# Twelve embedding tables looked up by matmul instead of ten, a 2 KB gather-descriptor ring, 25 chunks of marks, and whole layer parts between the gram pieces

## What is computed

```python
e = jnp.stack([tbl_0[ids[:, 0]], ..., tbl_25[ids[:, 25]]], axis=1)      # (2048, 26, 128)
combined = jnp.concatenate([dense[:, None, :], e], axis=1)              # (2048, 27, 128)
interactions = jnp.einsum('bfd,bgd->bfg', combined, combined)[:, TRIU_I, TRIU_J]   # 351
h = jnp.concatenate([dense, interactions, dense], axis=1)               # (2048, 607)
h = jnp.maximum(h @ W_top1 + b_top1, 0.0)
h = jnp.maximum(h @ W_top2 + b_top2, 0.0)
y = h @ W_top3                                                          # (2048, 1)
```

## Time and profile before

| | before |
|---|---|
| median of 3 runs | 398.69 us (398.37 to 398.92) |
| the profiled execution | 400.2 us, of which 398.3 us is the span of its instructions |
| PE busy / PE weight loads | 364.5 us (92%) / 309.7 us (78%) |
| DVE busy | 261.1 us (66%) |
| POOL busy | 247.2 us (62%), 256 gathers |
| ACT busy | 137.0 us (34%) |
| granted TensorE clock, mean | 0.983 of full speed |
| DMA | 31.72 MB, 80 GB/s on average |

### The profile page before, as it was taken

One profiled execution on the slowest core, in us unless ns is written; L12 is line 12 of the kernel. 1 busy time (PEld: TensorE's weight loads), 2 busy tenths in 40 slices (PEclk: granted clock), 3 DMA queues, 4 the chain that ended last, 5 costly groups with the idle time before them and its releaser, 6 DMA issues.

```text
span 398.3 us, 13947 instructions
## 1 busy us (share of the span) xinstructions
PE 364.5 (92%) x6192; PEld 309.7 (78%) x6192; DVE 261.1 (66%) x748; ACT 137.0 (34%) x195; POOL 247.2 (62%) x260
## 2 busy tenths in 40 slices
PE   0857758999999999999999999999999999999798
PEld 0757747987689977997789876997789877997575
DVE  2999864990699409990599519990699419980310
ACT  3545130343325234323433334323433334324222
POOL 6777777777677665776677666775677666720000
PEclk9998996999999999999999999999999999999989
DMA  7953442223112311323122311313121312200000
GB/s 242 411 195 110 149 144 57 54 55 120 49 42 55 113 43 44 82 53 115 43 55 55 114 49 44 81 54 109 48 51 53 116 47 51 54 22 2 5 2 0
DMA packets 13677, 31.72 MB, mean 80 GB/s; under 512 B 5301, under 2 KB 6205, under 8 KB 13618
## 3 DMA queue, kind: packets, MB, share of 16 engines
q0 software_dynamic: 8192, 16.79, 15.9%
q1 hardware_dynamic: 5426, 14.04, 9.7%
HBM read 30.81 MB, written 0.01 MB: 77 GB/s over the span
## 4 chain that ended last, share of the span: by engine, by line
PE 48%; DVE 44%; issue 4%; DMA 3%; ACT 1%; SPq 0%
DVE marks L580 37%; PE flip_ps L364 12%; PE mlp_ps L412 11%; PE gram_ps L386 9%; PE flip_ps L346 6%; PE mlp_ps L421 5%; PE mlp_ps L415 3%; DVE dots L558 3%; DVE lo L588 3%; DMA feats<-small_rows 1%; DMA id_cols<-ids_in_pairs 1%; DVE pair_dots L566 1%; PE mlp_ps L430 1%; PE pairs_ps L397 1%; ACT feats L622 0%
## 5 line engine op out<-in xcount | busy, mean ns | idle before, releaser
L328 POOL DMA_INDIRECT emb<-tbl,idx x256 | 247.0, 965 | 103.8 <-issue 55.8
L580 DVE TENSOR_SCALAR marks<-id_cols,row_no 125x256 fp32r<-125x256 int16 x688 | 211.5, 384 | 4.9 <-DMA id_cols<-ids_in_pairs 4.9
L364 PE MATMUL flip_ps<-marks,hi 125*128 125x256 f32 x688 | 172.2, 291 | 18.4 <-DVE marks L580 18.0
L364 PE MATMUL flip_ps<-marks,lo 125*128 125x256 f32 x688 | 167.9, 284 | 0.0
L364 PEld LDWEIGHTS flip_ps<-marks,hi 125*128 125x128 f32 x688 | 132.6, 193 | 26.0 <-issue 21.3
L364 PEld LDWEIGHTS flip_ps<-marks,lo 125*128 125x128 f32 x688 | 132.7, 193 | 0.0
L558 DVE STREAM_TRANSPOSE dots<-gram_ps 128x864 f32<-128x864 f32 (+1 forms) x32 | 25.2, 824 | 105.8 <-PE gram_ps L386 105.8
L622 ACT COPY feats<-flip_ps 128x512 f32<-128x512 f32 x40 | 46.7, 1167 | 124.4 <-PE flip_ps L364 119.4
L386 PEld LDWEIGHTS gram_ps<-feats 128*27 128x27 f32 x4096 | 43.0, 106 | 44.4 <-issue 43.3
L544 ACT COPY feats<-flip_ps 128x512 f32<-128x512 f32 x64 | 45.0, 725 | 64.9 <-PE flip_ps L346 62.8
L386 PE MATMUL gram_ps<-feats 128*27 128x27 f32 x4096 | 54.9, 192 | 10.2 <-issue 6.8
(11 more groups left out here) (23 smaller groups left out, 63.6 us busy)
## 6 DMA issues: line engine op xcount, KB each, us to landing
id_cols<-ids_in_pairs SPq DMA_DIRECT2D x7, 640.0 KB
emb<-tbl,idx POOLq DMA_INDIRECT x256, 2.5
feats<-small_rows SPq DMA_DIRECT2D x5, 512.0 KB, 7.5
dense_sb<-dense_columns SPq DMA_DIRECT2D x4, 256.0 KB, 9.2
w1p_sb<-w_pairs SPq DMA_DIRECT2D x1, 702.0 KB
hT<-small_rows SPq DMA_DIRECT2D x1, 640.0 KB, 12.6
w1p_sb<-small_rows SPq DMA_DIRECT2D x1, 640.0 KB, 14.5
dots<-small_rows SPq DMA_DIRECT2D x1, 640.0 KB, 4.0
```

The lines of the kernel that those rows point to most:

```text
L328: nc.gpsimd.indirect_dma_start(emb[:, v, (f - 1) * P:f * P], None, tables[order[f - 1]][:, :], bass.IndirectOffsetOnAxis(ap=idx[:, t, orde ...
L364: last = nc.tensor.matmul(flip_ps[:, m % FLIP_BANKS, 2 * (s % 2):2 * (s % 2) + 2, :], part[s][0:R[s], half * x + c, :], marks[0:R[s], MARK ...
L580: last = nc.vector.tensor_scalar(marks[0:R[s], MARKS_AT[h] + c, :], id_cols[0:R[s], s, :], row_no[0:R[s], s, half * x + c:half * x + c + 1 ...
```

## The change

- LOOKED_UP goes from 10 to 12: two tables with 1250 rows are no longer gathered but looked up. The look-ups of a pair have 106 chunks instead of 86, 14 tables are gathered (groups of 4, 4, 4 and 2), and there are six look-up groups instead of five.
- The SBUF kept for the descriptors of POOL's gathers goes from its default of 16 KB a partition to 2 KB (dynamic_dma_scratch_size).
- The ring of marks goes from 28 to 25 chunks; AHEAD, which follows from it, becomes 6 half-tables (24 chunks), and the half-tables fall to other places of the ring.
- The layers between the gram pieces are no longer cut: the gram pieces stand as piece, flip, piece, and then a whole layer. layer 4 of the last pair but one moves ahead of the last pair's odd gram pieces, and the third layer ahead of the last piece. ACT's order and the list of weighted places follow.

Two tables more than before have to wait for a place at the start: tables 10 and 11 go to the places of tables 7 and 8.

```diff
--- before.py
+++ after.py
...
 GROUP = 4
-LOOKED_UP = 10
+LOOKED_UP = 12
...
-MARK_CHUNKS = 28
+MARK_CHUNKS = 25
...
             places = [looks(h) for h in range(HALVES)] + part_of_layers(0)
-            places += [piece(even, 0)] + flips(odd, 0) + [piece(even, 1), piece(even, 2)] + flips(odd, 1)
-            places += part_of_layers(1) + [piece(even, 3), piece(even, 4)] + flips(odd, 2) + [piece(even, 5)]
-            places += part_of_layers(2) + [piece(even, 6)] + flips(odd, 3) + [piece(even, 7)] + part_of_layers(3)
-            places += [piece(odd, 0)] + flips(following, 0) + [piece(odd, 1)] + part_of_layers(4)
-            places += [piece(odd, 2)] + flips(following, 1) + [piece(odd, 3), piece(odd, 4)] + flips(following, 2)
-            places += part_of_layers(5) + [piece(odd, 5), piece(odd, 6)] + flips(following, 3)
-            return places + [piece(odd, 7)] + part_of_layers(6)
+            for k in range(GROUPS):
+                places += [piece(even, 2 * k)] + flips(odd, k) + [piece(even, 2 * k + 1)] + part_of_layers(k + 1)
+            places += [piece(odd, 0)] + flips(following, 0) + [piece(odd, 1)] + flips(following, 1)
+            places += [piece(odd, 2), piece(odd, 3)] + part_of_layers(H1C + 1) + [piece(odd, 4)]
+            places += flips(following, 2) + [piece(odd, 5)] + flips(following, 3) + [piece(odd, 6)]
+            return places + part_of_layers(H1C + H2C) + [piece(odd, 7)]
...
-            def layer(i, q, parts=range(4)):
+            def layer(i, q):
...
-                for c in parts:
-                    if q < H1C and c < CHUNKS:
-                        last = nc.tensor.matmul(bank, w1p_sb[0:CHUNK, c, q * P:(q + 1) * P],
-                                                xT[0:CHUNK, c, :, :], start=(c == 0), stop=False)
-                    elif q < H1C:
-                        last = nc.tensor.matmul(bank, w1d_sb[:, q * P:(q + 1) * P],
-                                                dense_sb[:, i % DENSE_PAIRS, :], start=False, stop=True)
-                    else:
+                if q < H1C:
+                    for c in range(CHUNKS):
+                        nc.tensor.matmul(bank, w1p_sb[0:CHUNK, c, q * P:(q + 1) * P],
+                                         xT[0:CHUNK, c, :, :], start=(c == 0), stop=False)
+                    last = nc.tensor.matmul(bank, w1d_sb[:, q * P:(q + 1) * P],
+                                            dense_sb[:, i % DENSE_PAIRS, :], start=False, stop=True)
+                else:
+                    for c in range(H1C):
                         if q == H1C:
 
                             pe.wait_ge(s_act, STEPS * i + c + 1)
                         last = nc.tensor.matmul(bank, w2_sb[:, c, (q - H1C) * P:(q - H1C + 1) * P],
                                                 h1T[:, c, :], start=(c == 0), stop=(c == H1C - 1))
-                if 3 in parts:
-                    last.then_inc(s_mm, 1)
-
-            def third_layer(i, parts=range(H2C)):
-                for c in parts:
+                last.then_inc(s_mm, 1)
+
+            def third_layer(i):
+                for c in range(H2C):
 
                     pe.wait_ge(s_act, STEPS * i + H1C + c + 1)
                     last = nc.tensor.matmul(mlp_ps[0:1, 0, 0:2 * P], w3_sb[:, c:c + 1], h2T[:, c, :],
                                             start=(c == 0), stop=(c == H2C - 1))
-                if H2C - 1 in parts:
...
                 layer(i - 1, 0)
-                gram(2 * i, 0)
-                flip(2 * i + 1, 0)
-                layer(i - 1, 1, range(0, 1))
-                gram(2 * i, 1)
-                layer(i - 1, 1, range(1, 3))
-                gram(2 * i, 2)
-                flip(2 * i + 1, 1)
-                layer(i - 1, 1, range(3, 4))
-                gram(2 * i, 3)
-                layer(i - 1, 2, range(0, 2))
-                gram(2 * i, 4)
-                flip(2 * i + 1, 2)
-                layer(i - 1, 2, range(2, 3))
-                gram(2 * i, 5)
-                layer(i - 1, 2, range(3, 4))
-                layer(i - 1, 3, range(0, 1))
-                gram(2 * i, 6)
-                flip(2 * i + 1, 3)
-                layer(i - 1, 3, range(1, 2))
-                gram(2 * i, 7)
-                layer(i - 1, 3, range(2, 4))
+                for k in range(GROUPS):
+                    gram(2 * i, 2 * k)
+                    flip(2 * i + 1, k)
+                    gram(2 * i, 2 * k + 1)
+                    if k + 1 < H1C:
+                        layer(i - 1, k + 1)
 
             def odd_gram(i):
 
@@ -478,27 +460,22 @@
                     if i + 1 >= EARLY:
                         flip(2 * i + 2, k)
 
-                layer(i - 1, 4, range(0, 2))
+                layer(i - 1, H1C)
                 gram(2 * i + 1, 0)
                 next_flip(0)
-                layer(i - 1, 4, range(2, 3))
                 gram(2 * i + 1, 1)
+                next_flip(1)
+                gram(2 * i + 1, 2)
                 pair_rows(2 * i)
-                layer(i - 1, 4, range(3, 4))
-                gram(2 * i + 1, 2)
-                next_flip(1)
-                layer(i - 1, 5, range(0, 1))
                 gram(2 * i + 1, 3)
-                layer(i - 1, 5, range(1, 3))
+                layer(i - 1, H1C + 1)
                 gram(2 * i + 1, 4)
                 next_flip(2)
-                layer(i - 1, 5, range(3, 4))
                 gram(2 * i + 1, 5)
-                third_layer(i - 1, range(0, 1))
+                next_flip(3)
                 gram(2 * i + 1, 6)
-                next_flip(3)
+                third_layer(i - 1)
                 gram(2 * i + 1, 7)
-                third_layer(i - 1, range(1, 2))
 
...
 
+            layer(last - 1, H1C)
             for part in range(PIECES):
                 gram(tiles - 1, part)
                 if part == 3:
                     pair_rows(tiles - 2)
-            layer(last - 1, 4)
-            layer(last - 1, 5)
+            layer(last - 1, H1C + 1)
             pair_rows(tiles - 1)
...
-                activate(i - 1, range(0, 1))
-                keep_all(2 * i + 1, range(0, 2))
-                activate(i - 1, range(1, 2))
-                keep_all(2 * i + 1, range(2, 3))
-                activate(i - 1, range(2, 3))
-                keep_all(2 * i + 1, range(3, GROUPS))
-                activate(i - 1, range(3, H1C))
+                for k in range(GROUPS):
+                    activate(i - 1, range(k, k + 1))
+                    keep_all(2 * i + 1, range(k, k + 1))
+                activate(i - 1, range(H1C, H1C + 1))
                 if i + 1 < pairs:
                     if i + 1 >= EARLY:
-                        keep_all(2 * i + 2, range(0, 1))
+                        keep_all(2 * i + 2, range(0, 2))
                     keep_pairs(2 * i)
-                    activate(i - 1, range(H1C, H1C + 1))
-                    if i + 1 >= EARLY:
-                        keep_all(2 * i + 2, range(1, 3))
                     activate(i - 1, range(H1C + 1, H1C + H2C))
                     if i + 1 >= EARLY:
-                        keep_all(2 * i + 2, range(3, GROUPS))
+                        keep_all(2 * i + 2, range(2, GROUPS))
                     keep_y(i - 1)
             keep_pairs(tiles - 2)
-            activate(pairs - 2, range(H1C, H1C + H2C))
+            activate(pairs - 2, range(H1C + 1, H1C + H2C))
...
-    nc = bacc.Bacc("TRN2", target_bir_lowering=False, num_devices=1)
+    nc = bacc.Bacc("TRN2", target_bir_lowering=False, num_devices=1, dynamic_dma_scratch_size=2048)
```

More of the change, by code:

```diff
@@ L82, in tower @@
     AHEAD = max(h for h in range(1, HALVES + 1) if sum(SIZES[:h]) <= MARK_CHUNKS)
-    assert CHUNKS == 3 and H1C == 4 and H2C == 2 and GROUPS == 4
+    assert H1C == GROUPS == 4 and H2C == 2 and PIECES == 2 * GROUPS
     ctx = ExitStack()
```

4 lines of the change are left out of this document (2 added, 2 removed).

## The result

The changed kernel takes 457.98 us (median of 4 runs, 456.77 to 458.80) against 398.81 us before (398.37 to 399.10): a ratio of 1.148, 95% interval 1.145 to 1.151. The prediction was 454.5 us with a range of 440 to 467. The profiled execution took 458.29 us, its span is 456.4 us, 58.1 us more than before.

The account below looks back on a forecast made before the run. PE and DVE were taken as balanced in the look-ups, PE alone as the bound elsewhere. Start +18.5, pairs 3 to 6 look-ups 4 x 5.9 and smaller terms sum to +55.8 us: 454.5 us, range 440 to 467.

Parts of the forecast that it names:

- The price of a mark: DVE's marks: 0.261 us for a mark by itself, plus 0.19 us for each gather beside the marks.
- Rival 2: DVE's marks: 0.31 us each however few gathers there are, some +10 us, 464 us; chance 0.18.
- the look-up parts of pairs 3 to 6: Steady pairs: look-up part 27.55 us against 21.64, +5.9 us a pair, bounded by DVE.
- about 13 beside the marks: Look-up part of pairs 3 to 6: 14.6 gathers fall into it, about 13 beside DVE's marks, adding 2.5 us.
- The stop: Start: DVE stands from 41.75 to 51.75 us, until PE has looked up table 6; 10 of the start's +18.5 us.
- Pair 1: Pair 1: 90 marks instead of 70 remain, 25.8 us, look-up part +4.0 us; its gram part +0.15.
- The even tile: Gram part, even tile: from 11.9 to 12.55 us on PE with half a layer more in it, +0.65.
- The tail: After the last odd tile: half of layers 4 and 5's 5.3 us lies in the wait for DVE's transposes, -2.6 us.
- Rival 1: Start: no stop of DVE or a short one, -10 us, 444 us; chance 0.14.
- rival 3: POOL's descriptor ring holds one gather: 96 us a pair for POOL, over 700 us; chance 0.03.
- rival 4: POOL's gathers set the pair, so fewer gathers gain up to 5.0 us a pair, 364 us; chance 0.02.
- rival 5: Two tables looked up but nothing else moved, DVE hidden everywhere: +35 us, 434 us; chance 0.03.

Follow-up runs that it names:

- a lead of 1.0: The changed kernel with PACE_LEAD = 1.0 instead of 0.7 of a pair for the gathers; 457.53 us, ratio 1.149 to the kernel before.
- the exchange of loads: The changed kernel with pair 1's row numbers asked for ahead of the weights of layers 1 and 2 in SP's queue; 458.58 us, ratio 1.153.

## Why the prediction was right, and where it was off

**The mechanism.** DVE's marks end the look-up parts: in pairs 3 to 7 they are done 1.34 us before the look-ups, the 1.35 of the prediction. But they do so by little. With ten tables and a ring of 42 chunks, where PE waits for no mark, the part takes 21.0 us. With twelve tables one part is PE's alone too: in pair 7 of the kernel with a lead of 1.0 the 82 marks take 21.6 us, PE waits for none, and the part takes 25.34 us. So PE's own work accounts for 4.3 us of the 4.6 to 5.4 by which the part grew, and against the 26.2 to 27.1 us of pairs 3 to 6 DVE costs 0.9 to 1.7 us a pair, the most that marks made earlier could give back. No run with twelve tables does that.

**The price of a mark** held: 22.58 us for 82 marks is 82 x 0.261 and 6 gathers of 0.2, and with no gather beside them (pair 7 with the lead of 1.0) 82 marks take 21.63 us, 0.264 each. In the records of the changed kernel 5 or 10 marks of such a run are longer than the others, by 0.14 to 0.21 us (a record of 342 ns becomes one of up to 544), where a gather falls on them. Rival 2, a mark of 0.31 us however few gathers there are, would have needed 25.4 us for 82 marks; 22.6 and 23.4 were measured, with 6 and 11 gathers beside them. The kernel with one late gather shows the same price: 8 gathers fewer beside 58 marks made them 1.8 us faster (16.25 us for 18.04). So against the Trainium skill (SBUF — State Buffer, SBUF: two separate sides), by which a VectorE instruction with one SBUF input, outside the two-port modes, and GpSimd don't block each other, both directions are seen here: 0.2 us of a mark for each gather, and gathers of 8 to 14 us.

**The term that was too big: the look-up parts of pairs 3 to 6.** Predicted 4 x 5.9 = 23.6 us, measured 4.6, 5.4, 4.6 and 5.4. The wrong step is "about 13 beside the marks": only 6 or 11 gathers met them, as one gather was shut out for the rest of the run. 7 gathers are 1.4 us, 2 are 0.4. What looks like harm (POOL busy 35 us longer) is what spares DVE 3.6 us, since PE did not yet wait for the gathers; in the kernel with the late gather it did, and lost 2.8 to 3.0 us in two pairs.

**The start.** The stop: 9.73 us for 10, its two ends within 0.3 us (42.03 and 51.76 for 41.75 and 51.75). Marks done at 66.35, predicted 65.75. The load behind it was 1.1 us longer than the 5.5 + 0.4 of the working, as much as the exchange of loads took away.

**The term that was left out: the gram after the start.** I had put it at nothing. It is 2.1 us, one more hole of 2 us among its matmuls. The clock of 0.50 isn't the reason, since the kernel before has it there too. I had allowed for such holes in the steady odd tiles and not in the first one.

**Pair 1.** +5.3 us for +4.0. Its 90 marks cost what they should (25.3 us for 25.8). The failed step is that the ring of 25 doesn't stop DVE, which the working had for the steady pairs and left out for pair 1: it stopped DVE there for 1.78 us.

**The even tile.** 3.22 us for piece, flip, piece and layer, and 12.55 us on PE (118.54 to 131.09 in pair 1), exactly the sum of the working; from the end of the look-ups to lay_out it is 12.71 to 12.95 us in pairs 3 to 6 (before 12.16), so +0.55 to +0.8 for +0.65. The odd tile came out 0.4 to 0.7 us shorter, not 0.3, so that the gram part of pairs 3 to 6 cost 0.2 us altogether for 1.4.

**The tail.** Predicted -2.6, measured 0.0. PE's last row:

```profile
430.55 1.29 PE L385 MATMUL gram_ps<-feats 128*27 128x27 f32 x125
434.11 0.24 PE L385 MATMUL gram_ps<-feats 128*27 128x27 f32 x3 [2.27 <-issue]
...
434.79 1.27 PE L385 MATMUL gram_ps<-feats 128*27 128x27 f32 x122
437.93 0.25 PE L385 MATMUL gram_ps<-feats 128*27 128x27 f32 x6 [1.87 <-issue]
```

Two holes, 2.27 and 1.87 us, where there was one of 1.82. The tail gave its 2.6 us (18.16 for 20.76), the odd tile ahead of it took them back. I had named such a hole as the upper bound for the steady odd tiles, where none appeared, and not for the row in which one already stood. With ten tables there is one hole of 1.30 us and the 2.6 us are kept.

Rival 1 falls by the stop of 9.73 us; rival 3 since one gather starts 1.25 us after the other with the small ring too; rival 4 since PE waits for no gather; rival 5 since the table has +58 us, not +35, with DVE's marks ending every look-up part. The sum was 2.3 us short of 58.1: 1.5 (start), 2.1 (gram), 1.3 and 0.5 (look-ups of pairs 1 and 7) and 2.6 us (last row) were missed on one side, 3.6 (look-ups of pairs 3 to 6), 1.2 (their gram parts), 0.6 and 0.5 (pairs 1 and 2) on the other. That the total came within 1% is luck: errors of 8 us one way and 6 the other nearly cancelled.

## What to carry to other kernels

Before work is moved from an idle engine to a bound one, ask which second engine it drags along: here two tables of 4.8 us of matmuls a pair brought 5.2 us of marks to DVE, whose marks already ended the part, and took the room for the marks made ahead. Then price the bound engine by itself: over 4 us a pair would have been lost even if the marks had cost nothing. Making DVE's work earlier, in its idle time, was worth 1% where the tables moved to PE cost 13% (51.4 of 398.3 us). In a start, an in-order engine that has a copy standing behind its last load turns that load into a stop for everyone who needs the copy's bank; put the copy first.

## What the runs showed of the hardware

- A gather that meets DVE's marks lengthens one of them by 0.20 us (342 to 544 ns), in a few cases by 0.14; a gather can also be held beside marks that come back to back, for 18.2 us in the longest case, and ends within 0.1 to 0.8 us of a break as small as a 0.06 us MEMSET. Two of them, of 9.2 us, ended while marks still came back to back. All such gathers of over 5 us began after POOL had paused for 1.2 us or more; but other pauses of 1.5 to 2.2 us beside the marks had a gather of 0.97 to 1.14 us behind them. What decides between the two stays open.
- Gram matmuls set close together (128, with their weight loads, in 1.3 us) now and then have a hole of 1.8 to 2.3 us behind them, in which PE runs nothing and waits for nothing that the profile shows. The kernel with the row numbers first in SP's queue differs from the changed one in nothing there, yet its last odd tile took 7.29 us for 9.44 and its tail 19.04 for 18.16: where the holes fall moves from kernel to kernel.
- After 4.0 us in which PE waited, its granted clock was 0.50 of full speed for 12 us (the changed kernel, 80 to 92 us), and after 2.52 us it was 0.50 too (the kernel before, 62 to 66 us).
